# A fused attention and feed-forward kernel on one core: folding the value and output weights with 32-row matmuls, rings of four tiles, and a 64-unit weight matrix laid out twice

## Reference

```python
queries = (query @ Wq + bq).reshape(B, L, H, E)        # B 16, L 1024, H 16, E 32
keys_flat = k @ Wk + bk                                # 32 patterns
values = (keys_flat @ Wv + bv).reshape(B, S, H, D)
A = sparsemax(scale * einsum('blhe,bshe->bhls', queries, keys))
out = einsum('bhls,bshd->blhd', A, values)
out = transpose(out, (0, 2, 1, 3)).reshape(B, L, H * D)   # a row is 16 places of one head
x = layernorm(x + out @ Wo + bo)
s = einsum('btd,dm->btm', x, Win) + bin_               # M 64
h = relu(s[..., None] * W1 + b1)                       # 16 inner units
g = einsum('btmh,mh->btm', h, W2) + b2
x = layernorm(x + einsum('btm,md->btd', g, Wout) + bout)
```

## Time and profile before

| what | value |
|---|---|
| median of 3 runs | 1581.36 us (1575.73 to 1583.24) |
| the profiled execution: time, span | 1570.85 us, 1569.1 us |
| TensorE | 1415.4 us busy (90%), mean granted clock 0.96 |
| VectorE, ScalarE | 1096.9 us (70%), 1105.0 us (70%) |
| GpSimd | 655.8 us (42%) |
| DMA | 258.50 MB, mean 165 GB/s |

### The profile page before, as it was taken

The page is one execution under the profiler, slowest core; times in us unless marked ns, Lnnn a source line. Parts: engine busy times, 40 slices in busy tenths (PEclk is TensorE's granted clock), DMA queues, the critical chain, the costliest instruction groups (busy, mean ns, idle before and its releaser), DMA issues. The chain is left out here.

```text
span 1569.1 us, 25895 instructions
## 1 busy us (share of the span) xinstructions
PE 1415.4 (90%) x6102; PEld 915.1 (58%) x6102; DVE 1096.9 (70%) x4547; ACT 1105.0 (70%) x2402; POOL 655.8 (42%) x1645
## 2 busy tenths in 40 slices
PE   6887388799999999999999999999999999889984
PEld 5444144466666666666666666666666666545542
DVE  2654754578877877878788777888778777834454
ACT  3443143367787887788887787878888878867784
POOL 1221022223454444545544554444544444544444
PEclk9998698899999999999999999999999999989995
DMA  4333033655555555455545555555545555446753
GB/s 133 124 104 97 27 108 108 187 183 162 169 189 189 186 179 177 165 189 189 188 157 174 189 172 172 176 189 189 182 174 177 175 189 189 162 162 232 251 157 72
DMA packets 91798, 258.50 MB, mean 165 GB/s; under 512 B 15651, under 2 KB 15651, under 8 KB 75206
## 3 DMA queue, kind: packets, MB, share of 16 engines
q1 hardware_dynamic: 91590, 256.39, 49.0%
HBM read 206.00 MB, written 50.33 MB: 163 GB/s over the span
## 5 line engine op out<-in xcount | busy, mean ns | idle before, releaser
L610 PE MATMUL bank<-G_sb,pT 128*128 128x512 f32 x1024 | 465.7, 598 | 0.0
L977 DVE MAX8 top<-bank 128x8 f32<-128x32 f32 x2048 | 212.5, 181 | 146.9 <-issue 124.3
L610 PEld LDWEIGHTS bank<-G_sb,pT 128*128 128x128 f32 x1024 | 186.7, 192 | 186.9 <-issue 186.9
L419 POOL TENSOR_TENSOR shift_sq<-sum,per_row_sq 128x1 f32<-128x1 f32 x256 | 99.8, 390 | 413.1 <-DVE y_sb L883 412.8
L1019 DVE SCALAR_TENSOR_TENSOR acc<-hinge,w2c,acc 128x512 f32<-128x512 f32 x224 | 167.3, 747 | 61.3 <-ACT hinge L721 54.3
L721 ACT ACTIVATE hinge<-s_sb,b1c,w1c 128x512 f32<-128x512 f32 x256 | 205.7, 807 | 0.0
L706 ACT ACTIVATE unread<-y_sb,shift_sq 128x512 bf16<-128x512 f32 x256 | 183.1, 715 | 24.9 <-POOL minus_mean L421 24.8
L540 PE MATMUL bank<-A_hi,xT_hi 128*128 128x512 f32 x512 | 200.5, 392 | 0.0
L541 PE MATMUL bank<-A_lo,xT_hi 128*128 128x512 f32 x512 | 200.4, 391 | 0.0
L542 PE MATMUL bank<-A_hi,xT_lo 128*128 128x512 f32 x512 | 200.1, 391 | 0.0
L444 POOL TENSOR_TENSOR side<-side 128x256 bf16<-128x256 bf16 x128 | 86.6, 676 | 240.8 <-ACT side L793 240.8
(11 more groups left out here) (122 smaller groups left out, 2644.2 us busy)
## 6 DMA issues: line engine op xcount, KB each, us to landing
G_sb<-G_of_heads SPq DMA_DIRECT2D x128, 1024.0 KB, 5.4
x_sb<-in_L_attn_query_dram SPq DMA_DIRECT2D x128, 256.0 KB, 4.7
y_sb<-in_L_attn_query_dram SPq DMA_DIRECT2D x256, 128.0 KB, 5.4
out_dram<-o_sb SPq DMA_DIRECT2D x256, 128.0 KB, 4.7
G_of_heads<-y_sb SPq DMA_DIRECT2D x64, 256.0 KB, 2.6
y_sb<-in_L_attn_Wk_dram SPq DMA_DIRECT2D x1, 1024.0 KB, 5.6
y_sb<-in_L_attn_Wq_dram SPq DMA_DIRECT2D x1, 1024.0 KB, 8.2
y_sb<-in_L_attn_Wv_dram SPq DMA_DIRECT2D x1, 1024.0 KB
```

Of the source, the lines that this page charges most:

```text
L419: nc.gpsimd.tensor_tensor(shift_sq[:, par:par + 1], total[:, par:par + 1], per_row_sq[:], ALU.mult).then_inc(s_mean, 1)
L610: mm = nc.tensor.matmul(o_ps[i % 2][:], pT[:, bass.ds(pair_place(turn, i) + (i % H * C + c) * P, P)], G_sb[:, i % GR, c, :], start=(c == 0 ...
L977: mx = nc.vector.max(top8[:, h, :], z_ps[i % 2][:, h * S:(h + 1) * S])
```

## The change

There are three edits.

1. *Fold.* V is written four times side by side per head (`V_rep`), and 16 matmuls against 32 columns of the identity transpose it and put it on all four row groups of 32 partitions at once (`VT_rep`, 128 x 512). A piece now is (four heads, c, a): a matmul with 32 rows, on partitions 32a to 32a+31, whose output has the four heads' 32 patterns on 128 partitions. The four a of a unit lie on four different groups of rows and go to four banks. `bo` is added once in 16 pieces. There are still 64 pieces, 64 copies out and 64 stores of 256 KB, but four per slot, in slots 1 to 16.
2. *Rings.* XR and OR are 4.
3. *The 64 units.* `Win_sb` and `bin_sb` hold the 64 units twice, so L618 writes 128 partitions and one 128 x 128 activation copies s out. Two more small loads are issued at the start.

```diff
-        XR, YR, OR, UR, HR = 2, 16, 2, 8, 2
+        XR, YR, OR, UR, HR = 4, 16, 4, 8, 2
...
-            k = 3 * (turn * UNROLL + j - 1) if isinstance(turn, int) else PIECES
-            return range(max(k, 0), max(min(k + 3, PIECES), 0))
+            unit = turn * UNROLL + j - 1
+            return range(HPC * unit, HPC * unit + HPC) if 0 <= unit < PIECES // HPC else range(0)
+
+        def piece(k):
+
+            return k // (HPC * C), k // HPC % C, k % HPC
...
+                    (Win_sb[:, :, half], Win.rearrange("(c p) m -> p c m", p=P)),
+                    (bin_sb[half, :], bin_.rearrange("(m a) -> m a", a=1)),
...
-                    h, c = k // C, k % C
+                    heads, c, a = piece(k)
                     sp.wait_ge(s_Gev, k + 1)
-                    sp.dma_start(G_dram[h, :, c * D:(c + 1) * D], y_sb[:, k % STAGES, :]).then_inc(
-                        s_Gst[k % STAGES], 16)
+                    sp.dma_start(G_dram[HPC * heads:HPC * heads + HPC, a * S:(a + 1) * S, c * D:(c + 1) * D],
+                                 y_sb[:, k % STAGES, :]).then_inc(s_Gst[k % STAGES], 16)
...
-                        mm = nc.tensor.matmul(ys_ps[0:M, 0:P], Win_sb[:, c, :], yT[:, c, :], start=(c == 0),
+                        mm = nc.tensor.matmul(ys_ps[:, 0:P], Win_sb[:, c, :], yT[:, c, :], start=(c == 0),
                                               stop=(c == C - 1))
...
+                    for h in range(H):
+                        mm = nc.tensor.matmul(G_ps[0][:, h * S:(h + 1) * S],
+                                              V_rep[:, h * P:(h + 1) * P],
+                                              ident[:, 0:S], start=True, stop=True)
+                    mm.then_inc(s_vT, 1)
                 for k in pieces(turn, j):
...
-                    if c == 0:
-                        nc.tensor.matmul(G_ps[k % C][:], first_place[:], bo_row[:], start=True, stop=False)
-                    nc.tensor.matmul(G_ps[k % C][:], VT_blk[:, h, :], Wo_sb[:, c, :], start=(c > 0),
-                                     stop=True).then_inc(s_Gmm, 1)
+                    heads, c, a = piece(k)
+                    rows = slice(a * E, (a + 1) * E)
+                    pe.wait_ge(s_vTc, 1)
+                    if k >= HPC:
+                        pe.wait_ge(s_Gev, k - HPC + 1)
+                    with_bo = c == 0 and a == 0
+                    if with_bo:
+                        nc.tensor.matmul(G_ps[a][:], ones_row, bo_row[:], start=True, stop=False)
+                    nc.tensor.matmul(G_ps[a][:], VT_rep[rows, heads * P:(heads + 1) * P], Wo_sb[rows, c, :],
+                                     start=not with_bo, stop=True).then_inc(s_Gmm, 1)
...
-                    for half in (slice(0, M), slice(M, P)):
-                        nc.scalar.activation(s_sb[half, par, q * P:(q + 1) * P], ys_ps[0:M, 0:P], ACT.Identity,
-                                             bias=bin_sb[:]).then_inc(s_sc, 1)
+                    nc.scalar.activation(s_sb[:, par, q * P:(q + 1) * P], ys_ps[:, 0:P], ACT.Identity,
+                                         bias=bin_sb[:]).then_inc(s_sc, 1)
```

More of the change, by code:

```diff
@@ L151, in build_kernel @@
         G_sb = sb("G_sb", [P, GR, C, D])
-        V_blk, VT_blk = (G_sb[:, r].rearrange("p c n -> p (c n)").rearrange("p (h n) -> p h n", h=H)
-                         for r in range(2))
+        V_rep, VT_rep = G_sb[:, 0].rearrange("p c n -> p (c n)"), G_sb[:, 1, 0, :]
         G_dram = nc.dram_tensor("G_of_heads", [H, P, C * D], F32, kind="Internal").ap()
@@ L158, in build_kernel @@
         bo_row = sb("bo_row", [1, D])
-        first_place = sb("first_place", [1, P])
-        Win_sb = sb("Win_sb", [P, C, M])
+        ones_row = sb("ones_row", [1, P])[:]
+        Win_sb = sb("Win_sb", [P, C, P])
         Wout_hi = sb("Wout_hi", [P, D], F32R)
@@ L163, in build_kernel @@
         bout_rows = sb("bout_rows", [P, D], F32R)
-        bin_sb = sb("bin_sb", [M, 1])
+        bin_sb = sb("bin_sb", [P, 1])
         w1c = sb("w1c", [P, KH])
@@ L191, in build_kernel @@
         bq_c = sb("bq_c", [P, C])
-        ones_row = above[0:1, 0:P]
         kpT4, keysT4 = (r.rearrange("p (c n) -> p c n", c=C) for r in (o_sb[:, 0, :], o_sb[:, 1, :]))
@@ L288, in pieces @@
         def pieces(turn, j):
-            k = 3 * (turn * UNROLL + j - 1) if isinstance(turn, int) else PIECES
-            return range(max(k, 0), max(min(k + 3, PIECES), 0))
+            unit = turn * UNROLL + j - 1
+            return range(HPC * unit, HPC * unit + HPC) if 0 <= unit < PIECES // HPC else range(0)
+        def piece(k):
+            return k // (HPC * C), k // HPC % C, k % HPC
         def group_of(turn, i):
             return turn * (UNROLL // GROUP) + i // GROUP
-        KEY_LOADS, Q_LOADS, WLOADS = 3, 2, 16
-        FILLS = 15 + S
-        CONSTS = FILLS + 5
+        KEY_LOADS, Q_LOADS, WLOADS = 3, 2, 18
+        FILLS = 13 + S
+        CONSTS = FILLS + 4
         @block.sync
@@ L350, in slot @@
                     if isinstance(turn, int) and base + i < H:
-                        if h < GR:
+                        if h == 0:
                             sp.wait_ge(s_Gmm, PIECES)
-                        for k in range(C * h, C * h + C):
-                            sp.wait_ge(s_Gst[k % STAGES], 16 * (k // STAGES + 1))
+                        if h % HPC == 0:
+                            for r in range(STAGES):
+                                sp.wait_ge(s_Gst[r], 16 * (h // HPC + 1) * (HPC * C // STAGES))
                     if not isinstance(turn, int) or base + i >= GR:
@@ L592, in slot @@
                     if not isinstance(turn, int) or base + i >= 1:
-                        pe.wait_ge(s_sc, 2 * (base + i))
+                        pe.wait_ge(s_sc, base + i)
                     for c in range(C):
@@ L635, in slot @@
                     nc.tensor.matmul(f_ps[:], acc_lo[:, here], Wout_hi[:], start=False, stop=True).then_inc(s_f, 1)
[L636 to L642, removed]
-                for k in pieces(turn, j):
-                    h, c = k // C, k % C
-                    if c == 0:
[L646 to L651, removed]
-                        nc.tensor.matmul(G_ps[k % C][:], first_place[:], bo_row[:], start=True, stop=False)
-                    nc.tensor.matmul(G_ps[k % C][:], VT_blk[:, h, :], Wo_sb[:, c, :], start=(c > 0),
-                                     stop=True).then_inc(s_Gmm, 1)
+                if turn == 0 and j == 0:
+                    for h in range(H):
[3 more added lines that the diff above has]
+                    mm.then_inc(s_vT, 1)
+                for k in pieces(turn, j):
+                    heads, c, a = piece(k)
[8 more added lines that the diff above has]
+                                     start=not with_bo, stop=True).then_inc(s_Gmm, 1)
             slots(pe, slot)
@@ L671, in _ @@
                     act.wait_ge(s_const, CONSTS)
[L672 to L675, removed]
+                    nc.scalar.copy(V_rep.rearrange("p (h a d) -> p h a d", h=H, a=HPC),
+                                   ps[:].rearrange("p (h d) -> p h d", h=H).unsqueeze(2).broadcast_to(
+                                       [P, H, HPC, E])).then_inc(s_sev, 1)
                 elif name == "WqT":
@@ L717, in make_hinge @@
                 if k == 0:
-                    act.wait_ge(s_sc, 2 * (base + lead + GROUP))
+                    act.wait_ge(s_sc, base + lead + GROUP)
                 if not isinstance(turn, int) or base + lead > 0 or k >= HR:
@@ L804, in slot @@
                 probabilities(turn, j, 1)
[L805 to L810, removed]
+                if turn == 0 and j == 0:
+                    act.wait_ge(s_vT, 1)
+                    nc.scalar.copy(VT_rep, G_ps[0][:]).then_inc(s_vTc, 1)
                 for k in pieces(turn, j):
@@ L814, in slot @@
                         act.wait_ge(s_Gst[k % STAGES], 16 * (k // STAGES))
-                    nc.scalar.copy(y_sb[:, k % STAGES, :], G_ps[k % C][:]).then_inc(s_Gev, 1)
+                    nc.scalar.copy(y_sb[:, k % STAGES, :], G_ps[k % HPC][:]).then_inc(s_Gev, 1)
             slots(act, slot)
```

9 lines of the change are left out of this document (2 added, 7 removed).

## The result

The changed kernel has a median of 1603.38 us (1603.21 to 1604.34, four runs); the kernel before, run beside it on the same chip, has 1582.30 (1575.73 to 1586.68). The ratio is 1.0138, with a 95% interval of 1.0102 to 1.0174: slower by 1.4%, where 1496 us was forecast, and outside the range of 1465 to 1545. The profiled execution has a span of 1602.5 us, against 1569.1 before. That one of the kernel before (1570.85 us) is faster than all the other runs of it here (the lowest is 1575.73), so the spans differ by 33.4 us and the medians by 21.1; what follows compares the profiles.

What follows compares the result with a forecast made beforehand. TensorE was taken to set the pace in the long stretch. Terms -38 - 18 - 9 - 22 = -87, less 2 us kept back for the start's loads, gave -85: from the median 1581.36 to 1496 us, range 1465 to 1545.

Steps and rivals of the forecast that it cites:

- Slots 1 to 16, four pieces each: Fold slots with four pieces: 8.5 to 8.6 us against 8.4, taken as 0 us in all, bounds -12 and +14.
- the ring of `o_sb`: Four places end ScalarE's waits for stores, shrinking TensorE's idle time: -18 us long stretch, -9 at the end with the copies.
- The units twice: All 128 tiles: 128-column matmuls avoid gaps at changes of shape, 0.30 us a tile on TensorE, -38 us, bounds -29 and -44.
- The ring of x: Four places for x_sb change nothing in the long stretch or slots 1 to 16; they work only with the fold's earlier end.
- Slots 17 to 22: No pieces, copies or stores of G there, so loads of x go ahead: -22 us, bounds -15 and -30.
- The start: One copy of V for four, sixteen matmuls for sixteen transposes, two more small loads: 0 us, bounds -3 and +3.
- The 32-row matmuls: In slots 1 to 16 a unit's eight records take five steps, 2.15 us, bounds 0.86 and 3.44.
- A: Rival: the 32-row matmuls don't run side by side, 3.44 us a unit, about +10, 1506 us; chance 0.23.
- B: Rival: VectorE takes over and new waits replace those removed; -47, 1534 us; chance 0.16.
- D: Rival: the wide weight load of the doubled units is not hidden; +26, 1607 us, the slower side; chance 0.05.
- C: Rival: the clock falls in slots 1 to 16, some 5 us a slot in half of them, +40, 1536 us; chance 0.09.

Runs made afterwards that it cites:

- e1: The changed kernel with the columns of the transposed V ordered (pattern, head), so stores run over 32 patterns outermost; 1458.03 us, ratio 0.9199.
- e5: The kernel before with the 64 units twice and both rings of four, but the old fold; 1483.59 us, ratio 0.9361.
- e4: The kernel before with only both rings (XR and OR) of four; 1523.22 us, ratio 0.9597.
- e3: The kernel before with only the 64 units laid out twice and one copy of s; 1562.35 us, ratio 0.9869.
- e4o: The kernel before with only the ring of `o_sb` at four; 1525.18 us, ratio 0.9615.
- e6: The changed kernel with stores ordered (pattern, head) and x for tile j + 2 issued in slot j ahead of its stores; 1417.12 us, ratio 0.8933.
- e8: The changed kernel with each store of a piece split into two stores of two heads, same bytes; 1749.4 us (one run).
- e7: The changed kernel, slow stores kept, with x for tile j + 2 issued in slot j ahead of its stores; 1472.2 us (one run).

## Why the prediction was wrong, point by point

- **The step that failed** is "Slots 1 to 16, four pieces each", and in it the sentences on the stores: "Against it stands one store more just ahead of x: 256 KB at the 208 GB/s of the busiest stretch are 1.26 us, if nothing of it is hidden; the bounds are 0 and 1.26, and I take 0.5" for that store alone. It was priced as one store more of the kind that stood there before. The edit also changed the DRAM side of all four from 128 rows to 4 x 32, and a rate for one shape says nothing of another. The runs show 10.3 us for a slot's four stores (1 MB at 102 GB/s), where e1's rate gives 3.7, and x behind them: +133.5 us where the bounds were -12 and +14. The shape was there to read in the order and in the diff; I read what moved, and not what the transfer had become. No rival had it, so the range had no room for it. With e1's mend, which leaves the number of pieces, the stretch is 2.3 us shorter than before, inside those bounds, and the whole takes 1458 us, 38 below the forecast. So the rest of the sum was sized too small, by the ring of `o_sb` above all (below), and 1458 is itself just outside the range of 1465 to 1545.
- **The units twice: right in mechanism, and worth what was said only with the rings.** 0.30 us a slot was forecast and 9.90 - 9.59 = 0.31 is what e5 gains over e4; alone it is 0.06 (e3), or 22 us of the 38 by medians. The starts, 3.44 and 0.89, were those forecast.
- **The ring of `o_sb`: right in mechanism, too small.** -18 us in the long stretch was a part of the idle time that TensorE shows. The ring gives 0.41 us a slot, 38 us (e4o), more than the 27.4 us of that idle time. TensorE's busy time fell too, from 921.6 to 911.0 us with the same matmuls (e4), so some of the waiting had stood in what the profile calls busy, and the idle time was no upper bound.
- **The ring of x: nothing, as said** (e4 against e4o). Issuing the load two tiles ahead gives 41 us (e1 to e6), and the change didn't do that.
- **Slots 17 to 22: -22 forecast, -13.0 after, -23.8 in e1.** The size was right; in the kernel after, this stretch still begins behind slow stores, and its clock is 0.76, against 0.85 in e1.
- **The start: 0 forecast with 3 either way, +4.8 measured.** I had taken the sixteen matmuls at no more than double 3.03 us. They are 32 records, and take 6.88 us, 3.9 more than the sixteen transposes; the scores behind them start at half clock, which costs another 1.3. The timeline of the start, after, for the earlier trace rows:

```profile
28.99 1.87 ACT L671 COPY G_sb<-bank 128x2048 f32<-128x2048 f32 x1 [4.09 <-PE bank L515]
31.72 6.88 PE L639 MATMUL bank<-ident,G_sb 128*128 128x32 f32 x32
```

- **The 32-row matmuls:** I had five steps and 2.15 us for a unit. It takes 1.14 us at full clock (e1) and 2.09 at half. The Trainium skill, "TensorE: Matmul & The Clock Gate", section "Measured speedup vs the span model", has four 32-row matmuls at 3.07 times the speed of serial ones. That gave an estimate of 1.1 us, and the trace agrees with it and not with my five steps; as the prediction said, the sum hardly hung on it.
- **The rivals.** A is false: they run side by side. B is false: the long stretch has 9.59 us a slot, and TensorE has no idle time in it, against VectorE's 741.3 us and 85.1 behind its checks. D is false: records of L618 stand 0.11 us apart at 128 columns. C saw half clock in the fold, which came, but as a result of the waits for x: over 50 to 110 us it is 0.69 in the changed kernel, and 0.97 in e6 without them. The kernel ended on D's side of the scale for a reason that none of the four had.

## What to carry to other kernels

When an edit changes the shape of a transfer, price it anew and start from its outermost dimension on both sides, before bytes and before counts; the mend may be as cheap as another order of the partitions (145 us here for two access patterns). A load that the next step waits for is to be issued ahead of the bulk stores of this step; the deeper ring of x gave nothing without that. Where a second limit stands beside the first, as the ring of `o_sb` did beside the matmuls, try the edits alone and together: 0.06, 0.41 and 0.72 us a slot.

## What the runs showed of the hardware

- A store's rate follows its outermost dimension on the DRAM side, with the same bytes in rows of the same 2 KB: 51 GB/s at 2 (share of the DMA engines 0.13), 102 at 4 (0.26), and 286 at 32 with x beside it (0.83). Divided by 2 and 4, that is some 25 GB/s for each such engine. The number of parts that land late goes with it: 2, 4 and, with 32 outermost, 16.
- A load over all sixteen engines that is issued behind such stores takes as long as they do, 11.45 us against 3.42, although by the share of 0.26 most of the engines stand idle meanwhile. Its parts land accordingly, twelve by 4.98 us after the issue and the last four 10.66 to 11.41 us after it, with the last store's. The trace doesn't name the engines; that the four are the same ones is read from these times, and from e8, where it is fourteen and two.
- With such stores queued, SP's issuing takes longer too: 8.64 us for four in e7, 2.48 in e1.
- The eight records of a unit's four 32-row matmuls take 1.14 us (e1), against 1.88 for four records, two pieces, of 128 rows before, and TensorE's clock holds at 0.97 over 60 us with them (e6). In e1 the first records of the four start within 0.02 us (61.70 to 61.72), and the second ones too, from 62.23 to 62.25.
